# Neighbour sums of a graph layer: two fp32r halves against three bf16 parts and plain fp32 rows

## The chip, the cores and the metric

One core of a Trainium2 chip runs one program that holds four layers. The metric is device time in microseconds (us), the median of the runs. TensorE is shown as PE (matmuls) and PEld (weight loads), VectorE as DVE, ScalarE as ACT, GpSimd as POOL and SyncE as SP, which issues the plain transfers.

## The reference

The program normalises the 6250 x 256 features, adds a relational graph layer, an attention gate with four experts, a neighbour layer and a slice-attention layer. The change lies in the neighbour layer alone:

```
h_self   = feat @ W_self
h_sparse = keep the 32 largest of each row of feat @ W_neigh, the rest 0
summed   = segment_sum(h_sparse[src], dst)          # 200000 edges, sorted by dst
x        = x + h_self + summed / max(deg, 1)
```

feat is the row-normalised x. src is uniform over 6250 nodes; dst is dense at the low nodes and thin at the high ones. All is float32.

## The kernel before

Nodes stand in 49 windows of 128 rows. Two functions, run one after the other with a barrier of all engines at the end of each, make the neighbour layer.

**sparse_table** (L3012) makes the table of kept values. For each window ACT normalises the rows (norm, L3214), PE turns them (L3193) and ACT copies the turned rows out (copy, L3220); PE multiplies by both weights at once (L3202: plain fp32, 512 columns, of which 256 are h_self and 256 h_neigh). ACT takes the 512 columns out of PSUM (L3248, n_full). DVE searches the 32 largest in groups of four windows: four rounds of MAX8 (L3139) and MATCH_REPLACE8 (L3144). ACT makes a 0/1 mask of it (hide, L3228), seven windows behind its own loop. POOL adds h_self to x (L3113) and multiplies the mask by the values (choose, L3103, n_sparse). DVE cuts the upper 20 bits of each kept value out (head, L3152) and POOL subtracts them from the value (part, L3107): two halves that add up to the value exactly. SP writes n_sparse to table2 (1 KB a row) and the halves to table3 (2 KB a row).

Every engine works through its list in the written order. ACT's list for window w is norm(w+2), copy(w+1), hide(w-7), then the values of window w out of PSUM; DVE's is one group of four windows after the other, with the heads of four earlier windows between.

**neighbour_sums** (L1494) adds the rows up in two ways at once:

- The first 1024 tiles of 128 edges ("counted blocks") never fetch a row for an edge. Per pair of tiles (a group, 512 of them) DVE makes one-hots of source and target (mark, L1625 and L1627), PE multiplies them (outer, L1669, bf16) into a table of counts, ACT copies the counts into e_times (L1583), SP loads 128 neighbouring rows of table3 into e_loads (L1572), and PE multiplies counts by rows (inner, L1685). A group spans DWINDOWS = 1, 1, 2, 3, 3, 4, 5 or 5 windows of targets, and there is a matmul for each window and each half. Groups of a narrow and a wide block alternate, six windows to two groups throughout: 512 groups x 3 windows x 2 halves = 3072 matmuls of 256 columns.
- The other 544 tiles are gathered: POOL issues one indirect DMA a tile (L1600), 128 rows of table3 of 2 KB each, into a ring of 12 tiles; DVE makes a one-hot of targets (L1647), and PE multiplies it by both halves (L1697), two matmuls of 256 columns a tile.

PE's written order goes by gathered tile: the matmuls of tile t, then for the groups placed at it (groups_at, spread evenly over the first 528 tiles) outer(g) and inner(g-2). Operands of L1685 and L1697 are typed float32r ("fp32r"): one matmul instruction each, where a plain fp32 matmul shows as two. Four PSUM banks hold the running totals of a couple of blocks; between couples DVE adds them to the accumulators (take, L1639 and L1642), and PE clears the banks by multiplying zeros (L1679).

Of the kernel before, what the change touches and what calls it, by code (L numbers as in the profile page):

```python
# [5 lines left out]
F32 = mybir.dt.float32  # L6
I32 = mybir.dt.int32
BF16 = mybir.dt.bfloat16
# [73 lines left out]
UPPER = -(1 << 12)  # L82
# [1411 lines left out]
def neighbour_sums(nc, b, table, halves):  # L1494
# [7 lines left out]
    RING = 12  # L1502
# [33 lines left out]
    with Phase(nc) as ctx:  # L1536
        sem = lambda name: ctx.semaphore(name)
        sb = lambda name, shape, dt=F32: ctx.enter_context(nc.sbuf_tensor(name, shape, dt))
        ring = sb("e2_ring", [P, RING, 2, D], F32R)
        onehot = [sb(f"e2_onehot{s}", [P, P], F32R) for s in range(ONEHOTS)]  # L1540
# [5 lines left out]
        times = [sb(f"e2_times{s}", [P, DWIDE * P], F32R) for s in range(TIMES)]  # L1546
        loads = sb("e2_loads", [P, AHEAD, 2, D], F32R)
# [17 lines left out]
        @block_ctx.sync  # L1565
        def _(eng):
            for g in range(GROUPS):
                of = edges_of(g)
                at = of % (BLOCKS // 2) * P + of // (BLOCKS // 2)
                low = eng.value_load(b.dfirst[0:1, at:at + 1], min_val=0, max_val=NP - P)  # L1570
                wait_if(eng, spread, g - AHEAD + 1)
                eng.dma_start(loads[:, g % AHEAD, :, :].rearrange("p n d -> p (n d)").bitcast(F32),  # L1572
                              halves[bass.ds(low, P), :]).then_inc(fetched[g % AHEAD], 16)
            for s in range(AHEAD):
                eng.wait_ge(fetched[s], 16 * (GROUPS // AHEAD))
# [12 lines left out]
        @block_ctx.gpsimd  # L1588
        def _(eng):
            eng.iota(rampw[:, :], pattern=[[1, DWIDE * P]], base=0, channel_multiplier=0,  # L1590
                     allow_small_or_imprecise_dtypes=True).then_inc(numbered, 1)
            eng.iota(rampr[:, :], pattern=[[1, P]], base=0, channel_multiplier=0,
                     allow_small_or_imprecise_dtypes=True).then_inc(numbered, 1)
            eng.memset(zeros[:, :], 0.0).then_inc(numbered, 1)

            for t in range(TILES):
                if t >= RING:
                    eng.wait_ge(summed, t - RING + 1)
                    eng.sem_inc(cleared, 1)
                eng.indirect_dma_start(ring[:, t % RING, :, :].rearrange("p n d -> p (n d)").bitcast(F32), None, halves, bass.IndirectOffsetOnAxis(  # L1600
                    ap=b.esrc[:, FROM + t:FROM + t + 1], axis=0)).then_inc(gathered[t % RING], 16)
# [61 lines left out]
        def _(eng):  # L1663
# [10 lines left out]
            def inner(g):  # L1674
                n, c = block(g), g // COUPLE
                if g % COUPLE == 0:
                    wait_if(eng, taken, TAKEN_BY[c])
                    for s in banks[c]:
                        eng.matmul(total[s][:, :, :].rearrange("p w d -> p (w d)"), zeros[:, 0:P], zeros[:, :],  # L1679
                                   start=True, stop=False, skip_group_check=True)  # L1680
                eng.wait_ge(copied, units[g + 1])
                eng.wait_ge(fetched[g % AHEAD], 16 * (g // AHEAD + 1))
                for q in range(DWINDOWS[n]):
                    for half in range(2):
                        mm = eng.matmul(part(n, q), times[g % TIMES][:, q * P:(q + 1) * P],  # L1685
                                        loads[:, g % AHEAD, half, :], start=False, stop=False, skip_group_check=True)
# [1325 lines left out]
def sparse_table(nc, b, m):  # L3012
# [15 lines left out]
    with Phase(nc) as ctx:  # L3028
# [5 lines left out]
        full = [sb(f"n_full{s}", [P, 2, D]) for s in range(WAYS)]  # L3034
# [4 lines left out]
        split = [sb(f"n_split{s}", [P, 2, D]) for s in range(WAYS)]  # L3039
# [8 lines left out]
        upper = ctx.enter_context(nc.psum_tensor("n_upper", [P, BANK], F32))  # L3048
        bounded = sem("n_bounded")
# [13 lines left out]
        added = sem("n_added")  # L3063
        cleared = sem("n_cleared")
        stored = [sem(f"n_stored{s}") for s in range(WAYS)]
        headed = sem("n_headed")
        parted = sem("n_parted")
        block = ctx.enter_context(nc.Block())
        table = m["table2"].rearrange("(w p) d -> w p d", p=P)
        halves = m["table3"].rearrange("(w p) (n d) -> w p n d", p=P, n=2)  # L3070

        @block.sync
        def _(eng):
# [11 lines left out]
            def body(few):  # L3085
                for w, q in few:
                    eng.wait_ge(chosen, w + 1)
                    eng.dma_start(table[w], sparse[q][:, :]).then_inc(stored[q], 16)
                    eng.wait_ge(headed, w + 1)
                    eng.wait_ge(parted, w + 1)  # L3090
                    eng.dma_start(halves[w], split[q][:, :, :]).then_inc(stored[q], 16)
# [7 lines left out]
        def _(eng):  # L3099
            def choose(w):  # L3100
                eng.wait_ge(masked, w + 1)
                wait_if(eng, stored[w % WAYS], 32 * (w // WAYS))
                eng.tensor_tensor(sparse[w % WAYS][:, :], mask[w % WAYS][:, :], full[w % WAYS][:, 1, :], ALU.mult).then_inc(chosen, 1)  # L3103

            def part(w):
                eng.wait_ge(headed, w + 1)
                eng.tensor_tensor(split[w % WAYS][:, 1, :], sparse[w % WAYS][:, :], split[w % WAYS][:, 0, :],  # L3107
                                  ALU.subtract).then_inc(parted, 1)

            eng.memset(less[:, :], -1.0).then_inc(cleared, 1)  # L3110
            for w in range(NW):
                eng.wait_ge(evacuated, w + 1)
                eng.tensor_tensor(b.x[:, w, :], b.x[:, w, :], full[w % WAYS][:, 0, :], ALU.add).then_inc(added, 1)  # L3113
                if w >= LATER:
                    choose(w - LATER)
                if w >= LATER + BEHIND:
                    part(w - LATER - BEHIND)
            for w in range(NW - LATER, NW):
                choose(w)
                part(w - BEHIND)  # L3120
            for w in range(NW - BEHIND, NW):
                part(w)
            eng.wait_ge(chosen, NW)
            eng.wait_ge(parted, NW)
            eng.wait_ge(added, NW)

        @block.vector
        def _(eng):
            def search(few):
# [3 lines left out]
                for r in range(ROUNDS):  # L3133
                    values = lambda q: full[q][:, 1, :] if r == 0 else left[q][:, :]
# [14 lines left out]
            def head(w):  # L3149
                eng.wait_ge(chosen, w + 1)  # L3150
                wait_if(eng, stored[w % WAYS], 32 * (w // WAYS))
                eng.tensor_tensor(split[w % WAYS][:, 0, :].bitcast(I32), sparse[w % WAYS][:, :].bitcast(I32),  # L3152
                                  upper[:, 0:D].bitcast(I32), ALU.bitwise_and).then_inc(headed, 1)

            def pair(i):
# [3 lines left out]
                if not isinstance(i, int) or i > 0:  # L3159
                    for w in range(WAYS * i - GROUP4, WAYS * i):  # L3160
                        head(w)
                search(here(GROUP4))
                for w in range(WAYS * i, WAYS * i + GROUP4):
                    head(w)
# [3 lines left out]
            eng.memset(upper[:, 0:D].bitcast(I32), UPPER).then_inc(bounded, 1)  # L3168
# [5 lines left out]
            eng.wait_ge(bounded, 1)  # L3174
# [4 lines left out]
            for w in range(NW - 1 - GROUP4, NW):  # L3179
                head(w)  # L3180
# [8 lines left out]
        def _(eng):  # L3189
# [6 lines left out]
            def body(w, s):  # L3196
# [14 lines left out]
        def _(eng):  # L3211
# [18 lines left out]

            eng.wait_ge(stated, STATED)
# [6 lines left out]
            for w in range(NW):  # L3238
# [8 lines left out]
                wait_if(eng, added, w - WAYS + 1)  # L3247
                eng.activation(full[w % WAYS][:, :, :].rearrange("p n d -> p (n d)"), product[w % 2][:, :],  # L3248
                               ACT.Copy).then_inc(evacuated, 1)
            for w in range(NW - LATER, NW):  # L3250
                hide(w)
# [494 lines left out]
def build(nc, m):  # L3746
# [3 lines left out]
    m["table3"] = nc.dram_tensor("table3", [NP, 2 * D], F32).ap()  # L3750
# [124 lines left out]
```

## Time and profile before

| | |
|---|---|
| time, median of 3 runs | 4351.2 us (4351.14 to 4359.82) |
| span of the profiled execution | 4349.6 us, mean granted clock 0.906 |
| sparse_table | 3010 to about 3195 us |
| neighbour_sums | about 3196 to 3951 us |
| PE busy over the span | 3703.0 us (85%) |
| moved by DMA over the span | 682.83 MB, mean 157 GB/s |

The profiled execution has no time of its own beside its span; the median of the runs is 1.6 us longer than the span, and what is added to the span is added to the median. Matmuls are pipelined: a matmul's duration in a row is longer than the distance to the next one, and it is the distance that says how many fit into a microsecond. A merged row of a timeline (x10) lasts from the first start to the last end.

### The profile page before, as it was taken

The page shows a single profiled execution, that of the slowest core. Times are in us where ns is not written, and L with a number is a line of the kernel's source. Part 1 is how long each engine was busy: PE and PEld are TensorE (multiplying, and loading weights), DVE is VectorE, ACT ScalarE, POOL GpSimd, SP SyncE. Part 2 cuts the span into 40 slices and gives each one's busy share as a digit, 9 for nine tenths or more (in the row PEclk, how much of TensorE's full clock was granted, in tenths as well). Part 3 has the DMA queues.
Part 4 walks back from the last instruction along what each step waited for, and adds up shares of the span by engine and source line. Part 5 has one row for each costly group of instructions (what it writes and reads, how often), then busy time and mean ns, then how long its engine had stood idle before and what let it go on. Part 6 is the DMA issues. An engine that isn't in the chain of part 4 may idle for free. (4 is left out here: it accounts for less than half of the span.)

```text
span 4349.6 us, 73406 instructions
## 1 busy us (share of the span) xinstructions
PE 3703.0 (85%) x19616; PEld 2744.7 (63%) x19641; DVE 2690.5 (62%) x9486; ACT 1684.8 (39%) x3943; POOL 2823.1 (65%) x2869
## 2 busy tenths in 40 slices
PE   4999996778777778877699999978769999996988
PEld 2566663444445556746588888866348888884657
DVE  8766656656544443445555455557978888886862
ACT  3444453434323333323344444446523333333320
POOL 5777777777777777772577777751667767672230
PEclk9999997776689999975799999999879999997998
DMA  7555553333434443531423323336379999993001
GB/s 252 188 193 186 188 191 119 105 105 105 115 115 124 125 123 106 164 105 43 91 66 69 69 66 70 70 101 213 117 279 385 368 367 385 373 385 95 1 1 59
DMA packets 354620, 682.83 MB, mean 157 GB/s; under 512 B 69218, under 2 KB 181104, under 8 KB 347853
## 3 DMA queue, kind: packets, MB, share of 16 engines
q0 software_dynamic: 133184, 338.60, 25.7%
q1 hardware_dynamic: 221039, 339.52, 23.1%
q8 instruction: 178, 2.92, 0.3%
q14 instruction: 219, 1.79, 0.1%
HBM read 565.53 MB, written 112.35 MB: 156 GB/s over the span
## 5 line engine op out<-in xcount | busy, mean ns | idle before, releaser
L1070 POOL DMA_INDIRECT e_ring<-table,erow x1040 | 1004.6, 966 | 316.9 <-issue 165.2
L1488 PE MATMUL e_sums<-e_ring,e_onehot 128*128 128x257 f32 x2080 | 821.2, 501 | 297.4 <-DMA e_ring<-table,erow 250.4
L2587 POOL DMA_INDIRECT t_source<-source_rows,t_index x632 | 606.9, 960 | 209.0 <-issue 157.2
L1488 PEld LDWEIGHTS e_sums<-e_ring,e_onehot 128*128 128x128 f32 x2080 | 379.7, 226 | 564.5 <-issue 332.6
L1600 POOL DMA_INDIRECT e_ring<-table,esrc x544 | 531.1, 976 | 212.9 <-issue 128.3
L560 POOL DMA_INDIRECT r_ring<-rows,esrc x400 | 449.7, 1124 | 149.7 <-issue 93.0
L1036 ACT ACTIVATE k_sign<-ramp,low 128x128 bf16<-128x128 f32 x1024 | 364.1, 395 | 447.9 <-PE e_sums L1459 429.7
L1685 PE MATMUL e_total<-e_loads,e_times 128*128 128x256 f32 x3072 | 502.7, 300 | 17.2 <-DMA e_loads<-table 12.3
L1685 PEld LDWEIGHTS e_total<-e_loads,e_times 128*128 128x128 f32 x3072 | 409.3, 190 | 69.5 <-issue 35.2
L1583 ACT ACTIVATE e_times<-e_tally 128x320 fp32r<-128x320 f32 (+4 forms) x640 | 259.7, 426 | 484.8 <-PE e_tally L1669 480.0
L2771 PE MATMUL t_raw<-big,t_w 128*128 128x256 f32 x1600 | 377.9, 390 | 20.2 <-ACT t_hidden L2606 19.4
L1305 DVE SCALAR_TENSOR_TENSOR big<-e_sums,within,big 128x257 f32 x130 | 63.0, 484 | 532.8 <-PE e_sums L1488 530.4
L738 PE MATMUL r_product<-weights,r_xt 128*128 128x512 f32 x784 | 372.0, 597 | 0.0
L2782 PE MATMUL t_out<-t_w,t_hidden 128*128 128x256 f32 x1600 | 368.2, 383 | 0.0
L2771 PEld LDWEIGHTS t_raw<-big,t_w 128*128 128x128 f32 x1600 | 301.8, 193 | 65.8 <-ACT t_hidden L2606 26.1
L1627 DVE TENSOR_SCALAR e_place<-e_rampw,ddst 128x128 bf16<-128x128 f16 (+4 forms) x1024 | 340.0, 334 | 0.0
L1625 DVE TENSOR_SCALAR e_row<-e_rampr,dsrc 128x128 bf16<-128x128 bf16 x1024 | 272.8, 268 | 95.9 <-PE e_tally L1669 84.5
L2782 PEld LDWEIGHTS t_out<-t_w,t_hidden 128*128 128x128 f32 x1600 | 297.7, 190 | 37.3
L1367 DVE TENSOR_SCALAR e_onehot<-ramp,edst 128x128 f32<-128x128 f32 x1040 | 247.0, 295 | 18.0 <-DVE d_keys L1092 2.2
L1669 PE MATMUL e_tally<-e_place,e_row 128*128 128x320 bf16 (+4 forms) x1258 | 255.4, 300 | 1.5
L1697 PE MATMUL e_sums<-e_ring,e_onehot 128*128 128x256 f32 x1088 | 202.0, 284 | 44.7 <-DMA e_ring<-table,esrc 44.6
L752 PE MATMUL r_sums<-r_ring,r_onehot 128*128 128x257 f32 x800 | 220.1, 385 | 19.2 <-DMA r_ring<-rows,esrc 19.1
(560 smaller groups left out, 6336.4 us busy)
## 6 DMA issues: line engine op xcount, KB each, us to landing
e_loads<-table SPq DMA_DIRECT2D x512, 256.0 KB
table<-r_stage SPq DMA_DIRECT2D x49, 1024.0 KB
outputs<-first_outputs SPq DMA_DIRECT2D x49, 512.0 KB, 6.6
first_outputs<-t_stage SPq DMA_DIRECT2D x96, 256.0 KB
t_near<-near_rows SPq DMA_DIRECT2D x79, 256.0 KB
e_ring<-table,erow POOLq DMA_INDIRECT x1040
table<-n_split SPq DMA_DIRECT2D x49, 256.0 KB
t_source<-source_rows,t_index POOLq DMA_INDIRECT x632
```

The lines of the kernel that those rows point to most:

```text
L560: eng.indirect_dma_start(ring[:, t % RING, 0:D], None, m["rows1"], bass.IndirectOffsetOnAxis(ap=b.esrc[:, SKIP + t:SKIP + t + 1], axis=0)) ...
L738: mm = eng.matmul(product[n % BANKS][:, :], xt[w % 2][:, k, :], b.weights[:, k, 2 * c:2 * c + 2, :].rearrange("p r o -> p (r o)"), start=( ...
L1036: eng.activation(sign[t % SIGNS][:, :], b.ramp[:, 0:P], ACT.Sign, bias=b.low[:, t:t + 1], scale=1.0).then_inc(signed, 1)
L1070: eng.indirect_dma_start(ring[:, t % RING, 0:D], None, table, bass.IndirectOffsetOnAxis(ap=b.erow[:, EARLY + t:EARLY + t + 1], axis=0)).th ...
L1488: eng.matmul(sums[g % SUMS][:, 0:ACCW], onehot[t % ONEHOTS][:, :], ring[:, t % RING, :], start=(t % GROUP == 0), stop=(t % GROUP == GROUP ...
L1600: eng.indirect_dma_start(ring[:, t % RING, :, :].rearrange("p n d -> p (n d)").bitcast(F32), None, halves, bass.IndirectOffsetOnAxis(ap=b. ...
L1625: eng.tensor_scalar(row[g % (MARKS // 2)][:, two, :], rampr[:, :], b.dsrc[:, column(tile):column(tile) + 1], None, ALU.is_equal).then_inc( ...
L1627: eng.tensor_scalar(place[(2 * g + two) % MARKS][:, 0:wide(g) * P], rampw[:, 0:wide(g) * P], b.ddst[:, column(tile):column(tile) + 1], Non ...
L1685: mm = eng.matmul(part(n, q), times[g % TIMES][:, q * P:(q + 1) * P], loads[:, g % AHEAD, half, :], start=False, stop=False, skip_group_ch ...
L2587: eng.indirect_dma_start(source[s][:, q, :], None, a.source_rows, bass.IndirectOffsetOnAxis(ap=index[s][:, q:q + 1], axis=0)).then_inc(gat ...
L2771: mm = eng.matmul(raw[g][:, j % 2, :], w1[:, e, k, j * P:(j + 1) * P], b.xt[:, k, bass.ds(w * P, PAIR)], start=(k == 0), stop=(k == KH - 1))
L2782: mm = eng.matmul(out[s][:, q, :], hidden[s][:, j, q * P:(q + 1) * P], w2[:, e, j, :], start=(j == 0), stop=(j == NB - 1))
```

## The change

The table for the neighbour sums is stored as three bf16 parts (first the value rounded to bf16, then the rest rounded, then what is left; 1.5 KB a row) in place of two fp32 halves. Counted blocks load these parts and multiply counts in bf16 by three parts. Gathered tiles take plain fp32 rows of table2 (1 KB) and plain fp32 one-hots: one fp32 matmul a tile. The ring has 24 tiles of 1 KB rows in place of 12 of 2 KB.

In sparse_table the parts are made by two ACT copies to bf16 (head, middle) and two POOL subtractions (remain, last); DVE's heads and POOL's addition to x are gone. x is added by PE instead (a matmul of the identity by x into the product's first 256 columns), and ACT takes the product out of PSUM in two pieces, one into x and one into n_full.

```diff
 def neighbour_sums
-    RING = 12
+    RING = 24
-        ring = sb("e2_ring", [P, RING, 2, D], F32R)
-        onehot = [sb(f"e2_onehot{s}", [P, P], F32R) for s in range(ONEHOTS)]
+        ring = sb("e2_ring", [P, RING, D])
+        onehot = [sb(f"e2_onehot{s}", [P, P]) for s in range(ONEHOTS)]
-        times = [sb(f"e2_times{s}", [P, DWIDE * P], F32R) for s in range(TIMES)]
-        loads = sb("e2_loads", [P, AHEAD, 2, D], F32R)
+        times = [sb(f"e2_times{s}", [P, DWIDE * P], BF16) for s in range(TIMES)]
+        loads = sb("e2_loads", [P, AHEAD, THIRDS, D], BF16)
...
-                eng.indirect_dma_start(ring[:, t % RING, :, :]..., None, halves, ...
+                eng.indirect_dma_start(ring[:, t % RING, :], None, table, ...
...
-                    for half in range(2):
+                    for third in range(THIRDS):
                         mm = eng.matmul(part(n, q), times[g % TIMES][:, q * P:(q + 1) * P],
-                                        loads[:, g % AHEAD, half, :], start=False, stop=False, skip_group_check=True)
+                                        loads[:, g % AHEAD, third, :], start=False, stop=False, skip_group_check=True)
...
-                for half in range(2):
-                    mm = eng.matmul(sums[g8 % 2][:, 0:D], onehot[t % ONEHOTS][:, :], ring[:, s, half, :],
-                                    start=(half == 0 and t % GROUP == 0), stop=(half == 1 and t % GROUP == GROUP - 1))
-                mm.then_inc(summed, 1)
+                eng.matmul(sums[g8 % 2][:, 0:D], onehot[t % ONEHOTS][:, :], ring[:, s, :],
+                           start=(t % GROUP == 0), stop=(t % GROUP == GROUP - 1)).then_inc(summed, 1)
 def sparse_table
         # gpsimd
-            for w in range(NW):
-                eng.wait_ge(evacuated, w + 1)
-                eng.tensor_tensor(b.x[:, w, :], b.x[:, w, :], full[w % WAYS][:, 0, :], ALU.add).then_inc(added, 1)
-                if w >= LATER:
-                    choose(w - LATER)
-                if w >= LATER + BEHIND:
-                    part(w - LATER - BEHIND)
+            for w in range(NW + 2):
+                if w < NW:
+                    choose(w)          # also waits for first of w - WAYS
+                if 1 <= w <= NW:
+                    remain(w - 1)      # rest = sparse - parts[0], waits for first
+                if w >= 2:
+                    last(w - 2)        # parts[2] = rest - parts[1], waits for second
         # vector: head(w) and its calls in pair(i) and at the end are gone
         # tensor, body(w, s)
                 wait_if(eng, evacuated, w - 1)
+                wait_if(eng, kept, w - 1)
                 for k in range(KH):
                     mm = eng.matmul(product[s][:, :], xt[s][:, k, :], ...
+                    if k == 0:
+                        eng.matmul(product[s][:, 0:D], b.ident[:, :], b.x[:, w, :], start=False, stop=False)
         # scalar
+            def head(w):
+                eng.wait_ge(chosen, w + 1)
+                wait_if(eng, stored[w % WAYS], 32 * (w // WAYS))
+                eng.activation(parts[w % WAYS][:, 0, :], sparse[w % WAYS][:, :], ACT.Copy).then_inc(first, 1)
+            def middle(w):
+                eng.wait_ge(rested, w + 1)
+                eng.activation(parts[w % WAYS][:, 1, :], rest[w % len(rest)][:, :], ACT.Copy).then_inc(second, 1)
+            def split(w):              # where in range: hide(w), head(w - 1), middle(w - 2)
...
-                if w >= LATER:
-                    hide(w - LATER)
+                split(w - LATER)
                 eng.wait_ge(multiplied, w + 1)
                 wait_if(eng, chosen, w - WAYS + 1)
-                eng.activation(full[w % WAYS][:, :, :]..., product[w % 2][:, :], ACT.Copy).then_inc(evacuated, 1)
+                eng.activation(b.x[:, w, :], product[w % 2][:, 0:D], ACT.Copy).then_inc(kept, 1)
+                eng.activation(full[w % WAYS][:, :], product[w % 2][:, D:2 * D], ACT.Copy).then_inc(evacuated, 1)
-            for w in range(NW - LATER, NW):
-                hide(w)
+            for w in range(NW - LATER, NW + 2):
+                split(w)
 def build
-    m["table3"] = nc.dram_tensor("table3", [NP, 2 * D], F32).ap()
+    m["table3"] = nc.dram_tensor("table3", [NP, THIRDS * D], BF16).ap()
```

## Rows read from the trace of the kernel before

**Rows 1.** The page: busy us (share of the span) of each engine; DMA busy tenths

```profile
PE 3703.0 (85%) x19616; PEld 2744.7 (63%) x19641; DVE 2690.5 (62%) x9486; ACT 1684.8 (39%) x3943; POOL 2823.1 (65%) x2869
...
DMA  7555553333434443531423323336379999993001
```

**Rows 2.** Busy us by stretch: PE, PEld, DVE, ACT, POOL; PE clock, DMA share, GB/s

```profile
3010.00:3195.50 185.50, 115.46 (x294) 50.38 (x294) 163.01 (x649) 87.85 (x198) 103.52 (x148) 0.83 0.34 122
...
3202.40:3946.60 744.20, 709.91 (x5428) 615.80 (x5452) 621.33 (x2729) 259.73 (x640) 527.17 (x541) 0.99 1.02 372
```

**Rows 3.** Groups in 3202.4 to 3946.6 us: busy us, mean ns, idle before, releasers

```profile
L1600 POOL DMA_INDIRECT e_ring<-table,esrc x541 | 527.6, 975 | 212.1 <-issue 127.6 <-PE e_sums L1697 84.5
L1685 PE MATMUL e_total<-e_loads,e_times 128*128 128x256 f32 x3072 | 502.7, 300 | 17.2 <-DMA e_loads<-table 12.3 <-ACT e_times L1583 3.2
L1685 PEld LDWEIGHTS e_total<-e_loads,e_times 128*128 128x128 f32 x3072 | 409.3, 190 | 69.5 <-issue 35.2 <-ACT e_times L1583 17.1
...
L1697 PE MATMUL e_sums<-e_ring,e_onehot 128*128 128x256 f32 x1088 | 202.0, 284 | 44.7 <-DMA e_ring<-table,esrc 44.6
```

**Rows 4.** Timeline of PE around 3351 us: start, us, line, count

```profile
3350.19 1.46 PE L1685 MATMUL e_total<-e_loads,e_times 128*128 128x256 f32 x10
3351.49 0.64 PE L1697 MATMUL e_sums<-e_ring,e_onehot 128*128 128x256 f32 x4
3351.97 0.29 PE L1669 MATMUL e_tally<-e_place,e_row 128*128 128x128 bf16 x2
3352.07 0.48 PE L1685 MATMUL e_total<-e_loads,e_times 128*128 128x256 f32 x2
3352.39 0.74 PE L1669 MATMUL e_tally<-e_place,e_row 128*128 128x320 bf16 x4
3352.86 1.46 PE L1685 MATMUL e_total<-e_loads,e_times 128*128 128x256 f32 x10
```

**Rows 5.** Timeline of PE elsewhere: fp32 of 256 columns, bf16 of 20, 512 and 384

```profile
2508.52 3.62 PE L2782 MATMUL t_out<-t_w,t_hidden 128*128 128x256 f32 x16
...
2511.97 0.75 PE L2758 MATMUL gsums<-t_parts,t_place 128*128 128x20 bf16 x24
...
3758.40 0.82 PE L1679 MATMUL e_total<-e_zeros 128*128 128x512 bf16 x3 [2.95 <-DVE big L1642]
...
1298.82 0.49 PE L1444 MATMUL d_keys<-d_target,d_half 128*128 128x384 bf16 x2
```

**Rows 6.** One line's durations, ns min/median/max: L1444, L2782

```profile
L1444 PE MATMUL d_keys<-d_target,d_half x128: 322/326/528, 1235.2 to 1639.2; 128*128 128x384 bf16 x128
...
L2782 PE MATMUL t_out<-t_w,t_hidden x1600: 378/379/463, 2123.2 to 2911.1; 128*128 128x256 f32 x178
```

**Rows 7.** Groups in 3010 to 3195.5 us: busy us, mean ns, idle before, releasers

```profile
L3144 DVE MATCH_REPLACE8 n_left<-n_best,n_left 128x256 f32<-128x256 f32 x147 | 58.5, 409 | 0.0
...
L3214 ACT ACTIVATE n_xn<-features,shift,rstd 128x256 f32<-128x256 f32 x49 | 28.8, 590 | 0.8 <-DVE shift L3173 0.8
L3228 ACT ACTIVATE n_mask<-n_left,n_less 128x256 f32<-128x256 f32 x49 | 24.3, 503 | 60.8 <-DVEq L3147 60.8
...
L3220 ACT ACTIVATE n_xt<-n_turned 128x256 f32<-128x256 f32 x49 | 18.2, 371 | 1.2 <-PE n_turned L3194 1.2
...
L3152 DVE TENSOR_TENSOR n_split<-n_sparse,n_upper 128x256 int32<-128x256 int32 x49 | 17.3, 414 | 2.5 <-DVE n_left L3144 2.0 <-POOL n_sparse L3103 0.2
```

**Rows 8.** Timeline of DVE and ACT in sparse_table: start, us, line, count

```profile
3154.10 1.41 DVE L3152 TENSOR_TENSOR n_split<-n_sparse,n_upper 128x256 int32<-128x256 int32 x4 [0.22 <-DVE n_left L3144]
...
3167.26 1.41 DVE L3152 TENSOR_TENSOR n_split<-n_sparse,n_upper 128x256 int32<-128x256 int32 x4 [0.22 <-DVE n_left L3144]
...
3168.59 1.40 DVE L3139 MAX8 n_best<-n_full 128x8 f32<-128x256 f32 x4
...
3179.11 1.71 ACT L3228 ACTIVATE n_mask<-n_left,n_less 128x256 f32<-128x256 f32 x4 [9.21 <-DVEq L3147]
```

More of the change, by code:

```diff
@@ L81 @@
 TAKEN = -2.0 ** 127
-UPPER = -(1 << 12)
+THIRDS = 3
 SH, SD, SG = 8, 64, 64
@@ L1491, in _, with neighbour_sums @@
                     tally(t)
-def neighbour_sums(nc, b, table, halves):
+def neighbour_sums(nc, b, table, thirds):
     ONEHOTS = BODY
-    RING = 12
+    RING = 24
     MARKS = 8
@@ L1571, in _ @@
                 wait_if(eng, spread, g - AHEAD + 1)
-                eng.dma_start(loads[:, g % AHEAD, :, :].rearrange("p n d -> p (n d)").bitcast(F32),
-                              halves[bass.ds(low, P), :]).then_inc(fetched[g % AHEAD], 16)
+                eng.dma_start(loads[:, g % AHEAD, :, :].rearrange("p n d -> p (n d)"),
+                              thirds[bass.ds(low, P), :]).then_inc(fetched[g % AHEAD], 16)
             for s in range(AHEAD):
@@ L1599, in _ @@
                     eng.sem_inc(cleared, 1)
-                eng.indirect_dma_start(ring[:, t % RING, :, :].rearrange("p n d -> p (n d)").bitcast(F32), None, halves, bass.IndirectOffsetOnAxis(
+                eng.indirect_dma_start(ring[:, t % RING, :], None, table, bass.IndirectOffsetOnAxis(
                     ap=b.esrc[:, FROM + t:FROM + t + 1], axis=0)).then_inc(gathered[t % RING], 16)
@@ L3033, in sparse_table @@
         xt = [sb(f"n_xt{s}", [P, KH, P]) for s in range(2)]
-        full = [sb(f"n_full{s}", [P, 2, D]) for s in range(WAYS)]
+        full = [sb(f"n_full{s}", [P, D]) for s in range(WAYS)]
         left = [sb(f"n_left{s}", [P, D]) for s in range(WAYS)]
@@ L3038, in sparse_table @@
         sparse = [sb(f"n_sparse{s}", [P, D]) for s in range(WAYS)]
-        split = [sb(f"n_split{s}", [P, 2, D]) for s in range(WAYS)]
+        parts = [sb(f"n_parts{s}", [P, THIRDS, D], BF16) for s in range(WAYS)]
+        rest = [sb(f"n_rest{s}", [P, D]) for s in range(WAYS // 2)]
         less = sb("n_less", [P, 1])
@@ L3047, in sparse_table @@
         product = [ctx.enter_context(nc.psum_tensor(f"n_product{s}", [P, BANK], F32)) for s in range(2)]
-        upper = ctx.enter_context(nc.psum_tensor("n_upper", [P, BANK], F32))
-        bounded = sem("n_bounded")
         loaded = sem("n_loaded")
@@ L3062, in sparse_table @@
         chosen = sem("n_chosen")
-        added = sem("n_added")
+        kept = sem("n_kept")
         cleared = sem("n_cleared")
         stored = [sem(f"n_stored{s}") for s in range(WAYS)]
-        headed = sem("n_headed")
-        parted = sem("n_parted")
+        first = sem("n_first")
+        rested = sem("n_rested")
+        second = sem("n_second")
+        third = sem("n_third")
         block = ctx.enter_context(nc.Block())
         table = m["table2"].rearrange("(w p) d -> w p d", p=P)
-        halves = m["table3"].rearrange("(w p) (n d) -> w p n d", p=P, n=2)
+        thirds = m["table3"].rearrange("(w p) (n d) -> w p n d", p=P, n=THIRDS)
         @block.sync
@@ L3088, in body @@
                     eng.dma_start(table[w], sparse[q][:, :]).then_inc(stored[q], 16)
-                    eng.wait_ge(headed, w + 1)
-                    eng.wait_ge(parted, w + 1)
-                    eng.dma_start(halves[w], split[q][:, :, :]).then_inc(stored[q], 16)
+                    eng.wait_ge(second, w + 1)
+                    eng.wait_ge(third, w + 1)
+                    eng.dma_start(thirds[w], parts[q][:, :, :]).then_inc(stored[q], 16)
             each_few(eng, body)
@@ L3101, in choose, with remain, last @@
                 eng.wait_ge(masked, w + 1)
+                wait_if(eng, first, w - WAYS + 1)
                 wait_if(eng, stored[w % WAYS], 32 * (w // WAYS))
[L3103 to L3108, printed above, removed]
-            eng.memset(less[:, :], -1.0).then_inc(cleared, 1)
-            for w in range(NW):
-                eng.wait_ge(evacuated, w + 1)
-                eng.tensor_tensor(b.x[:, w, :], b.x[:, w, :], full[w % WAYS][:, 0, :], ALU.add).then_inc(added, 1)
-                if w >= LATER:
-                    choose(w - LATER)
-                if w >= LATER + BEHIND:
-                    part(w - LATER - BEHIND)
-            for w in range(NW - LATER, NW):
[L3119 to L3125, printed above, removed]
+                eng.tensor_tensor(sparse[w % WAYS][:, :], mask[w % WAYS][:, :], full[w % WAYS][:, :], ALU.mult).then_inc(chosen, 1)
+            def remain(w):
+                eng.wait_ge(first, w + 1)
+                wait_if(eng, third, w - len(rest) + 1)
+                eng.tensor_tensor(rest[w % len(rest)][:, :], sparse[w % WAYS][:, :], parts[w % WAYS][:, 0, :],
+                                  ALU.subtract).then_inc(rested, 1)
+            def last(w):
+                eng.wait_ge(second, w + 1)
+                eng.tensor_tensor(parts[w % WAYS][:, 2, :], rest[w % len(rest)][:, :], parts[w % WAYS][:, 1, :],
+                                  ALU.subtract).then_inc(third, 1)
+            eng.memset(less[:, :], -1.0).then_inc(cleared, 1)
+            for w in range(NW + 2):
[5 more added lines that the diff above has]
+                    last(w - 2)
+            eng.wait_ge(third, NW)
         @block.vector
@@ L3133, in search @@
                 for r in range(ROUNDS):
-                    values = lambda q: full[q][:, 1, :] if r == 0 else left[q][:, :]
+                    values = lambda q: full[q][:, :] if r == 0 else left[q][:, :]
                     for w, q in few:
@@ L3147, in search @@
                     eng.sem_inc(searched, 1)
[L3149 to L3153, printed above, removed]
             def pair(i):
@@ L3158, in pair @@
                 search(here(0))
-                if not isinstance(i, int) or i > 0:
-                    for w in range(WAYS * i - GROUP4, WAYS * i):
-                        head(w)
                 search(here(GROUP4))
-                for w in range(WAYS * i, WAYS * i + GROUP4):
-                    head(w)
             s = Chain(eng, stated)
             variances(eng, s, b, b.counts, work)
-            eng.memset(upper[:, 0:D].bitcast(I32), UPPER).then_inc(bounded, 1)
             eng.wait_ge(rooted, 1)
@@ L3173, in _ @@
             r.did(eng.scalar_tensor_tensor(b.shift[:, :], b.mean[:, :], -1.0, b.rstd[:, :], ALU.mult, ALU.mult))
-            eng.wait_ge(bounded, 1)
             pair(0)
@@ L3178, in _ @@
             search([(NW - 1, 0)])
-            for w in range(NW - 1 - GROUP4, NW):
-                head(w)
             eng.wait_ge(brought, 128)
@@ L3229, in hide @@
                                scale=-2.0 ** -126).then_inc(masked, 1)
+            def head(w):
[6 more added lines that the diff above has]
+            def split(w):
+                if w >= 0 and w < NW:
+                    hide(w)
+                if w - 1 >= 0 and w - 1 < NW:
+                    head(w - 1)
+                if w - 2 >= 0 and w - 2 < NW:
+                    middle(w - 2)
             eng.wait_ge(stated, STATED)
@@ L3242, in _ @@
                     copy(w + 1)
-                if w >= LATER:
-                    hide(w - LATER)
+                split(w - LATER)
                 eng.wait_ge(multiplied, w + 1)
                 wait_if(eng, chosen, w - WAYS + 1)
[L3247 to L3250, printed above, removed]
-                hide(w)
+                eng.activation(b.x[:, w, :], product[w % 2][:, 0:D], ACT.Copy).then_inc(kept, 1)
+                eng.activation(full[w % WAYS][:, :], product[w % 2][:, D:2 * D], ACT.Copy).then_inc(evacuated, 1)
+            for w in range(NW - LATER, NW + 2):
+                split(w)
+            eng.wait_ge(kept, NW)
 def attention_phase(nc, b, m):
```

## The prediction

> **What bounds the kernel now.** I read the page first: PE is the busiest engine (85%), and DMA is full in the fourth quarter of the span alone [rows 1]. That quarter is the neighbour sums, so the stretches come next [rows 2]. In the 744.2 us from the first to the last matmul of that stage PE is shown busy for 710, DMA for 102% at 372 GB/s, DVE for 621, POOL for 527 and ACT for 260. Two things look full, so the question is which of them the stage would keep if the other were relieved. The idle times say little against PE: it waited 17 us for loads and counts, and 45 us for gathered rows, of which some 38 lie ahead of the first one [rows 3]. The timeline settles it. One turn of PE's list, two groups with two gathered tiles, runs from 3350.19 to 3352.86 without a shown wait, 2.67 us [rows 4]. There are 256 such turns, with 528 tiles between them (2.06 a turn), and 16 tiles behind the last. At 0.24 us for a tile's two matmuls (four in 0.48, from 3351.49 to 3351.97) that is 256 x (2.67 + 0.0625 x 0.24) = 687, and 4 for the last tiles: 691 of 744 us are PE's own issue. The other 53 are waits: about 5 at the start, 3 at each of the three changes of couple (one stands in the rows [rows 5]: 2.95 us for DVE ahead of the zeros), 8 in the last tiles, and some 31 scattered ones.
>
> So transfers and PE are nearly level, PE slightly ahead. In sparse_table it is DVE: 163 of 185 us [rows 2], in groups of four windows 13.16 us apart (3154.10 to 3167.26) [rows 8].
>
> **Counted blocks.** Per turn six windows get three matmuls in place of two: 18 for 12, of 256 columns each. The old ones go at 0.119 us: four of the same shape last 0.64 with a last one of 0.284, (0.64 - 0.28) / 3 [rows 3, 4]. A bf16 matmul of 256 columns behind another is what the trace of before doesn't show in such a run, so I bound it. Below: a pair of 384 columns lasts 0.49 with a second of 0.326, 0.164 apart [rows 5, 6], which is 0.43 ns a column, or 0.109 for 256. Above: 0.12, no better than the fp32r matmuls that it replaces. Which end holds hangs on the weights, loaded anew for each matmul. An fp32r load takes 0.190 [rows 3] and sits beside every 0.119 step; the bf16 matmuls of 20 columns, each with its load, follow at (0.75 - 0.17) / 23 = 0.025 [rows 5] (0.17 for the last one), so bf16 loads need not slow a 0.109 step. I take 0.109 and keep 0.12 as the upper end. Per turn 18 x 0.109 - 12 x 0.119 = +0.53 us, over 256 turns +137 (at 0.12: +187).
>
> The Trainium skill, "TensorE: Matmul & The Clock Gate", section "Back-to-back issue gap", has a warm gap of columns / 2.4 GHz plus 2.5 ns, 109 ns here, but also says that streams of weight load and matmul are set by both. With its first figure the sum is the same; its caution is what the upper end stands for.
>
> **Gathered tiles.** A plain fp32 matmul is two instructions: 16 of them, 256 columns wide, last 3.62 with a last one of 0.379, (3.62 - 0.38) / 15 = 0.216 apart [rows 5, 6]. A tile costs 0.432 for 0.238, +0.194, and 544 tiles +105 us. This price is the trace's own; I give it no spread.
>
> **What gets cheaper.** Bytes: 512 loads fall from 256 to 192 KB (134 to 101 MB) and 544 gathers from 256 to 128 KB (143 to 71 MB), 172 for 277 MB. Over a stage that is longer, DMA stands under half. Of the 53 us of waits, the scattered 31 go almost entirely, I leave 3; the 8 in the last tiles go, since PE then takes 0.43 us a tile with 24 of them fetched ahead; start and couple changes stay. So minus 36. POOL issues as many gathers: 528 busy and 128 of issue for 541 [rows 3], 1.21 us each, 659 us in all, no bound under a longer stage, and nor are DVE's 621 or ACT's 260. ACT's copies of counts keep their number and shape.
>
> Sum for the stage: 744 + 137 + 105 - 36 = 950, **+206 us**. Nothing of another stage lies beside it (a barrier on both sides), so all of it reaches the end.
>
> **The table stage.** DVE's four heads a group go: from 3167.26 to 3168.59 1.33 us, with 0.22 of wait ahead [rows 8], 1.55 a group, 17 us for eleven groups; the five at the end (0.33 each) stood before POOL's last parts, and I count 1. Whether DVE can use it depends on ACT's list, which grows by two copies of SBUF rows (near L3228: 0.503 long, (1.71 - 0.50) / 3 = 0.40 apart) and one more PSUM copy (L3220: 0.371) [rows 7, 8]. Per window that is at most 0.59 + 0.37 + 3 x 0.50 + 2 x 0.37 = 3.2 us by whole durations, some 2.5 by distances; DVE's group without heads is 11.6, 2.9 a window. The wait that matters: behind hide (which waits for the first window of a search to end) now stand head, middle and the copy into x before the last window of the next group gets out of PSUM, 0.50 + 0.40 + 0.40 + 0.30 + 0.37 = 2.0 us. DVE meanwhile has three more replaces (0.41 each, [rows 7]) and three MAX8 (0.35 each, from four in 1.40 [rows 8]), 2.3 us, so about 0 to 0.3 of wait a group, I take 2 us in all. At the start PE paces the first four windows, and the identity matmul adds 2 x 0.216 to each: +2. POOL trades three operations for three. At the end ACT's hide of the last window stands ahead of head and middle of the two before, a chain of six short steps against POOL's five queued parts before; I call it even. SP stores smaller parts, two transfers a window as before. The other new waits are met earlier: PE's for the copy into x by its wait for n_full, which ACT fills right after; POOL's choose waits for a head eight windows back, with choose, remain and last queued behind it. Together **-14 us**, between -20 and +10.
>
> Span 4349.6 + 206 - 14 = 4541.6, and with the 1.6 us by which the median of the runs exceeds the span, **4543 us**.
>
> **Rival 1: bf16 steps of 0.12.** Then 18 x 0.011 x 256 = 51 us more, 4594. For it: each matmul has weights of its own, and the steps in this very stage are 0.12 [rows 4]. Against it: the 384-column pair and the 20-column run. 24%.
>
> **Rival 2: the stage is bound by transfers and gets faster.** For it: DMA at 102% [rows 2]. If bytes alone set the time, 172 MB at 372 GB/s are 462 us; POOL's 659 us would then end last, with 10 of start and end a stage of 669, -75, and with the table stage 4351 - 75 - 14 = 4262. Against it: 691 us of issue. It decides only where a turn's matmuls fit into 2.6 us; with 0.72 for the tallies (2.67 less 12 x 0.119 and 0.48) and 2 x 0.43 for the tiles, a bf16 matmul would have to take (2.6 - 0.72 - 0.86) / 18 = 0.057 us, half of 0.109. 4%.
>
> The Trainium skill, "DMA: Bandwidth & Descriptors", section "Specifications", puts a core's HBM limit near 358 GB/s. The stage measured 372, so by that rule it is at the ceiling, and cutting bytes is what would pay; that is this rival's reading. [...]
>
> **Rival 3: the table stage becomes ACT's.** If ACT's activations follow each other by whole durations, a group takes 4 x 3.2 = 12.8 and the 2.0 us chain no longer hides: 15 us for 13.16, +22 over twelve groups in place of -14, 4579. Against it: four hides in 1.71 us [rows 8]. 9%.
>
> **How the numbers follow.** Forecast 62%, its own range 4518 to 4565 (no scattered waits and -20 in the table; 10 us more of waits and 0 there, with a step between the two bounds). With rivals 1 and 3 the range is 4515 to 4608, which leaves out rival 2 and the far ends, under 2 in 10. 0.2% is about what a measurement of this kernel can tell from no change. Faster is rival 2, 4%; no case lands within 0.2%, 1% for what I haven't thought of; slower 95%.
>
> **What would show it.** In the changed profile: L1685's counterpart x4608 at 0.109 in runs of 15 between two others; the gathered tiles x1088 as fp32, 0.216 apart; DMA share in the stage near one half; POOL waiting for PE at most gathers, its ring full; DVE's idle time in front of its one-hots or marks, put down to PE; the stage some 950 us from first to last matmul. In the table stage: groups 11.6 to 12 us apart, no int32 operation on DVE. A stage under 900 us, or PE waiting for e_ring or e_loads throughout, would make the prediction wrong, as would a bf16 step well under 0.1 us.

## The result and the profile after

The changed kernel takes 4515.66 us (median of 4 runs, 4514.36 to 4518.29), the kernel before 4351.17 in the same set: a ratio of 1.0375, 95% interval 1.0362 to 1.0387, 164 us slower. The forecast was 4543, 192 slower. The direction came out as forecast, and none of the three rivals did; the size is 27 us off. The measured time lies at the very low end of the range, 4515, and its interval reaches to 4509.

The page of the changed kernel, the lines that answer to [rows 1]: busy us by engine, and DMA's busy tenths in 40 slices.

```profile
PE 3933.8 (87%) x21239; PEld 2892.8 (64%) x21275; DVE 2675.8 (59%) x9436; ACT 1716.6 (38%) x4090; POOL 2807.3 (62%) x2869
...
DMA  7555553333444433523232333363666666672001
```

The nines of DMA in the fourth quarter have become sixes. The two stretches of [rows 2] in the changed kernel, busy us of PE, PEld, DVE, ACT and POOL, clock, DMA share and GB/s:

```profile
3010.00:3182.00 172.00, 126.09 (x392) 67.00 (x392) 147.06 (x599) 119.25 (x345) 97.49 (x148) 0.88 0.33 113
3188.30:4109.30 921.00, 910.73 (x6953) 735.54 (x6988) 624.93 (x2733) 259.22 (x640) 520.54 (x542) 1.00 0.65 188
```

From the first to the last matmul the neighbour sums take 921 us for 744, +177 where +206 was forecast. DMA moves half of the former GB/s, but is still busy for 0.65 of the time, where the working had it under half; PE is busy for 911 of 921. The groups that answer to [rows 3] (busy us, mean ns, idle before and its releasers):

```profile
L1685 PE MATMUL e_total<-e_loads,e_times 128*128 128x256 bf16 x4608 | 586.9, 273 | 0.0
L1600 POOL DMA_INDIRECT e_ring<-table,esrc x542 | 521.0, 961 | 380.0 <-PE e_sums L1696 283.0 <-issue 97.0
L1685 PEld LDWEIGHTS e_total<-e_loads,e_times 128*128 128x128 bf16 x4608 | 445.9, 98 | 84.8 <-issue 0.6
L1696 PE MATMUL e_sums<-e_ring,e_onehot 128*128 128x256 f32 x1088 | 306.7, 381 | 32.9 <-DMA e_ring<-table,esrc 32.9
```

PE never waits for loads or counts (0.0), and for a gathered row only ahead of the first tile (one wait of 32.9). POOL waits for PE 283 us in all: its ring is full. One turn of PE's list, to be laid beside [rows 4] (start, us, line, count):

```profile
3302.49 0.71 PE L1669 MATMUL e_tally<-e_place,e_row 128*128 128x320 bf16 x4
3303.03 1.80 PE L1685 MATMUL e_total<-e_loads,e_times 128*128 128x256 bf16 x15
3304.67 1.03 PE L1696 MATMUL e_sums<-e_ring,e_onehot 128*128 128x256 f32 x4
3305.54 0.28 PE L1669 MATMUL e_tally<-e_place,e_row 128*128 128x128 bf16 x2
3305.65 0.49 PE L1685 MATMUL e_total<-e_loads,e_times 128*128 128x256 bf16 x3
3305.98 0.71 PE L1669 MATMUL e_tally<-e_place,e_row 128*128 128x320 bf16 x4
```

From one group of tallies to the next, 3302.49 to 3305.98, a turn is 3.49 us, where the working gave 2.67 + 0.53 + 0.39 = 3.59. The bf16 step is (1.80 - 0.27) / 14 = 0.109, the fp32 one (1.03 - 0.38) / 3 = 0.217: both prices were right. So this tenth of a microsecond must lie in what was left at its old price. It is missing in the turns of the first two couples of blocks; those of the last two are a case of their own, taken up further down.

In the table stage the searches of DVE follow each other without heads (start, us; to be laid beside [rows 8]):

```profile
3145.02 1.41 DVE L3138 MAX8 n_best<-n_full 128x8 f32<-128x256 f32 x4 [0.29 <-DVE n_left L3143]
...
3156.92 1.41 DVE L3138 MAX8 n_best<-n_full 128x8 f32<-128x256 f32 x4 [0.28 <-DVE n_left L3143]
```

A group takes 11.90 us for 13.16, and the profile puts DVE's wait down to its own replaces, not to ACT. By the first and the last instruction the stage is 169.3 us for 180.4, -11 where -14 was forecast. With +177 in the sums and some 3 us less over barriers and other stages that is the 163.1 by which the span grew.

### The profile page after: what moved, and what is told of

The parts are those of the page before. It is cut to its first block and busy times, and to the rows that moved or that the text cites. A ratio compares the mean times of both kernels' runs of the same rounds, so it can differ in the third digit from the quotient of the medians.

```text
span 4512.7 us, 76792 instructions
## 1 busy us (share of the span) xinstructions
PE 3933.8 (87%) x21239; PEld 2892.8 (64%) x21275; DVE 2675.8 (59%) x9436; ACT 1716.6 (38%) x4090; POOL 2807.3 (62%) x2869
## 5 line engine op out<-in xcount | busy, mean ns | idle before, releaser
L1488 PE MATMUL e_sums<-e_ring,e_onehot 128*128 128x257 f32 x2080 | 838.0, 510 | 279.7 <-DMA e_ring<-table,erow 233.5
L1685 PE MATMUL e_total<-e_loads,e_times 128*128 128x256 bf16 x4608 | 586.9, 273 | 0.0
L1583 ACT ACTIVATE e_times<-e_tally 128x320 bf16<-128x320 f32 (+4 forms) x640 | 259.2, 425 | 661.4 <-PE e_tally L1669 658.4
L1685 PEld LDWEIGHTS e_total<-e_loads,e_times 128*128 128x128 bf16 x4608 | 445.9, 98 | 84.8 <-issue 0.6
L1696 PE MATMUL e_sums<-e_ring,e_onehot 128*128 128x256 f32 x1088 | 306.7, 381 | 32.9 <-DMA e_ring<-table,esrc 32.9
L1627 DVE TENSOR_SCALAR e_place<-e_rampw,ddst 128x128 bf16<-128x128 f16 (+4 forms) x1024 | 327.9, 321 | 0.0
L1669 PE MATMUL e_tally<-e_place,e_row 128*128 128x320 bf16 (+4 forms) x1248 | 245.3, 293 | 1.8
```

The source lines that it names most:

```text
L1488: eng.matmul(sums[g % SUMS][:, 0:ACCW], onehot[t % ONEHOTS][:, :], ring[:, t % RING, :], start=(t % GROUP == 0), stop=(t % GROUP == GROUP ...
L1627: eng.tensor_scalar(place[(2 * g + two) % MARKS][:, 0:wide(g) * P], rampw[:, 0:wide(g) * P], b.ddst[:, column(tile):column(tile) + 1], Non ...
```

## The experiments

**Gathered tiles alone.** The kernel before with one part of the change:

```diff
 # kernel before, neighbour_sums
-    RING = 12
+    RING = 24
-        ring = sb("e2_ring", [P, RING, 2, D], F32R)
+        ring = sb("e2_ring", [P, RING, D])
-        onehot = [sb(..., [P, P], F32R) ...]
+        onehot = [sb(..., [P, P]) ...]
         # gather from table in place of halves; one fp32 matmul a tile in place of two fp32r
```

> The kernel before with the gathered tiles alone as in the changed kernel: plain fp32 rows of 1 KB, fp32 one-hots, ring of 24; counted blocks keep their fp32r halves. Theory (PE's issue bounds the stage): a tile's matmuls go from 0.238 to 0.432 us, 544 x 0.194 = +105, and some 36 us of waits go with the bytes (205 for 277 MB) and the deeper ring: 4420 us. If the waits of the kernel before were not made by transfers, only the 8 us of the last tiles go: 4448. If transfers bounded the stage before (rival 2), the stage follows bytes down to PE's new issue of about 796 and no further: also near 4420, but then DMA, not PE, must have been what the stage before waited for; the run with half loads tells these apart.

Measured: 4397.24 us, ratio 1.0109 (1.0094 to 1.0123), +49. The stretch from the first to the last matmul of its sums:

```profile
3196.60:3992.60 796.00, 788.24 (x5451) 670.66 (x5452) 621.34 (x2731) 259.98 (x640) 518.29 (x541) 0.99 0.84 259
```

The stretch is 796 us for 744. The theory's +69 is too much by 20. Either more waits went than the 36 counted, or the tiles cost less than 105; with the next run the two can be told apart.

**Half of the loads.** The kernel before, moving less and multiplying as much:

```diff
 # kernel before, neighbour_sums
-        loads = sb("e2_loads", [P, AHEAD, 2, D], F32R)
+        loads = sb("e2_loads", [P, AHEAD, D], F32R)
-                eng.dma_start(loads[:, g % AHEAD, :, :]..., halves[bass.ds(low, P), :])
+                eng.dma_start(loads[:, g % AHEAD, :].bitcast(F32), table[bass.ds(low, P), :])
-                                        loads[:, g % AHEAD, half, :], ...
+                                        loads[:, g % AHEAD, :], ...
```

> The kernel before with loads of 128 KB in place of 256 for the counted blocks (rows of the whole values, the same 1 KB multiplied twice): the same matmuls, 210 for 277 MB. The counted sums come out doubled and unsplit. Theory: PE issues as before, 691 us, and only the scattered waits that transfers made can go: 15 to 31 us, 4320 to 4336. Rival (transfers bound the stage before): the stage falls to POOL's 659 and some 16 at the ends, 4282. Rival (the scattered waits are PE's own or ACT's): under 5 us, 4347 or more.

Measured: 4312.10 us, ratio 0.9914 (0.9902 to 0.9927), -36. Stretch and the group of the counted matmuls:

```profile
3194.30:3903.00 708.70, 692.08 (x5452) 622.91 (x5452) 616.58 (x2732) 259.64 (x640) 530.15 (x542) 0.98 0.91 297
```

```profile
L1685 PE MATMUL e_total<-e_loads,e_times 128*128 128x256 f32 x3072 | 509.6, 302 | 0.0
```

The stage stands at 709, not at 675: PE's issue was the wall behind the transfers, and transfers cost 35 us in front of it (15 to 31 were expected here, and the prediction let 28 of the scattered waits go). Rival 2 falls.

This run and the one before it move about as much (210 and 205 MB), so between them lies the price of the gathered tiles: 796.0 - 708.7 = +87, the shorter tail taken in (forecast: 105 - 8 = 97). By the starts of the matmuls in the two traces the tiles themselves cost the full 105; the waits in the last tiles shrink by some 12 and not 8, and the tally pairs behind a tile by 5 (the run with fp32r below takes these up). From the kernel with gathered fp32 tiles to the changed one lies the price of the counted blocks: 921 - 796 = +125 (forecast: 137).

**Two of three parts.** The changed kernel, a third of the counted matmuls left out:

```diff
 # changed kernel, inner
-                    for third in range(THIRDS):
+                    for third in range(2):
```

> The changed kernel with the third part left out of the multiplication (it is still made, stored and loaded): 3072 bf16 matmuls for 4608. Leaves out the lowest part of the values of the counted blocks. Theory: 1536 x 0.109 = 168 us less, 4348, the stage 753 us, since POOL's 659 and DVE's 621 stay below. Rival (something else stands close behind PE, ACT's copies of counts or POOL's issue): less falls away, 4370 or more, with PE waiting for e_times or e_ring.

Measured: 4355.39 us, ratio to the kernel before 1.0016 (1.0007 to 1.0025), so 160 below the changed kernel in place of 168. Its sums and the one new wait:

```profile
3182.30:3944.30 762.00, 754.03 (x5451) 586.34 (x5452) 620.66 (x2731) 259.16 (x640) 519.40 (x542) 0.99 0.76 226
```

```profile
PEld e_tally L1669 <- ACT e_times L1583: 18.9, 69, 0.5
```

921 - 762 = 159. The 1536 matmuls are worth 0.104 us each, nearly their whole step. Most of the other 9 us are a wait that stood behind: with a shorter inner the tallies of a wide block catch up with ACT's copies (18.9 us in 69 waits, where the changed kernel has 11.8 in 70), and turns are 2.83 or 2.94 us long. The rival is right about a neighbour close behind PE, and wrong about its size.

**What fp32r does to its neighbours.** The changed kernel with one fp32r matmul a tile:

```diff
 # changed kernel, neighbour_sums
-        ring = sb("e2_ring", [P, RING, D])
-        onehot = [sb(f"e2_onehot{s}", [P, P]) for s in range(ONEHOTS)]
+        ring = sb("e2_ring", [P, RING, D], F32R)
+        onehot = [sb(f"e2_onehot{s}", [P, P], F32R) for s in range(ONEHOTS)]
```

> The changed kernel with rows and one-hots of the gathered tiles typed float32r, so that a tile is one matmul at that precision instead of a plain fp32 one; leaves out the lower bits of the gathered values. Theory (an fp32r matmul makes the matmuls around it dearer): the tallies that follow a gathered tile show 0.067, 0.120 and 0.173 for 128, 256 and 384 columns between the two of a pair, as in the kernel before, where the changed kernel has 0.056, 0.109 and 0.162; the tile itself 0.12 in place of 0.432; 544 x 0.31 = 170 less and 5 to 10 back, 4351 to 4356. Rival (the dearer tallies of the kernel before came from its heavier transfers): tallies stay at 0.056, 0.109 and 0.162, 4346.

Measured: 4359.60 us, ratio to the kernel before 1.0021 (1.0012 to 1.0031). What decides is the distance between the starts of the two matmuls of a tally pair (outer makes one for each of a group's two tiles; the median of all 128, 64 and 128 pairs of a trace, in ns; L1669, bf16):

| columns | before | half loads | gathered fp32 | changed | gathered fp32r |
|---|---|---|---|---|---|
| 128 | 67 | 67 | 56 | 56 | 67 |
| 256 | 120 | 120 | 109 | 109 | 120 |
| 384 | 173 | 173 | 162 | 162 | 173 |
| what runs ahead of the pair | fp32r | fp32r | fp32 | fp32 | fp32r |

Eleven ns come and go with the type of the matmul ahead of the pair, not with the transfers: half the loads change nothing, and the last column has them back at the bytes of the changed kernel. Where bf16 runs ahead (the version with two bf16 parts, below) it is 56, 109 and 162 again. The pair itself starts on time, 122 ns after a tile's last fp32r matmul in the kernel before and 216 after its last fp32 one in the changed kernel, so the 11 ns are added to the turn. The dearer neighbours are shown. The median turn of this run, 2.88 us, is what these prices give (3.49 - 2 x 0.312 + 0.022 = 2.89); the total is 4 to 8 us above what was expected, so that lies in waits, which I haven't traced.

**The ring.** The changed kernel with 12 tiles:

```diff
-    RING = 24
+    RING = 12
```

> The changed kernel with a ring of 12 tiles in place of 24. Theory (PE's issue ends last and gathers are early): no difference, 4515 within 4. Rival (the deeper ring covers late gathers, above all in the last 16 tiles): 5 to 15 us more, PE waiting for e_ring.

Measured: 4517.63 us, ratio to the kernel before 1.0379 (1.0361 to 1.0397), against 1.0375: in the total, no difference that can be told. The trace does show the rival's wait, though. PE waits for gathered rows four times, and in the changed kernel once:

```profile
  DMA e_ring<-table,esrc: 34.8, 4
```

The three new waits (0.8, 1.5 and 1.0 us) stand ahead of the last four tiles, and the matmuls behind the last counted one take some 5 us longer; from first to last matmul the stage is 928 us for 921, while the whole span is 3.9 longer. So the deeper ring does cover late gathers at the end, as the prediction had it; the medians of the runs, 2 us apart with ranges that overlap, don't show it.

**The table stage alone.** The kernel before, with DVE's cut moved to ACT and the sums as they were:

```diff
 # kernel before, sparse_table
-        split = [sb(f"n_split{s}", [P, 2, D]) for s in range(WAYS)]
+        split = [sb(f"n_split{s}", [P, 2, D], F32R) for s in range(WAYS)]
         # vector: head(w) and its calls are gone
+            def head(w):               # scalar, called one window behind hide
+                eng.wait_ge(chosen, w + 1)
+                wait_if(eng, stored[w % WAYS], 32 * (w // WAYS))
+                eng.activation(split[w % WAYS][:, 0, :], sparse[w % WAYS][:, :], ACT.Copy).then_inc(headed, 1)
         # x added by PE's identity matmul, PSUM taken out in two pieces, as in the changed kernel
         # gpsimd: choose(w), then part(w - 1)
```

> The kernel before with the table stage alone changed: ACT rounds the kept values into the upper half (typed float32r) in place of DVE's cut, POOL subtracts as before, and x is added by PE's identity matmul. The neighbour sums are untouched. Theory (DVE bounds the table stage): 11 to 14 us less, 4338 to 4340, faster than both kernels. Rival (ACT's longer list takes over): no gain or up to 20 us more.

Measured: 4334.98 us, ratio 0.9964 (0.9951 to 0.9977), -13.5: faster than both kernels, with the values still split into two halves that add up to them. Its searches:

```profile
3143.93 1.41 DVE L3131 MAX8 n_best<-n_full 128x8 f32<-128x256 f32 x4 [0.29 <-ACT n_full L3238]
...
3155.83 1.41 DVE L3131 MAX8 n_best<-n_full 128x8 f32<-128x256 f32 x4 [0.28 <-ACT n_full L3238]
```

A group takes 11.90 us, as in the changed kernel, which makes one ACT copy and one POOL operation a window more. The profile puts the wait down to ACT here and to DVE there, but it is 0.28 to 0.29 us in both, whatever the length of ACT's list. So neither ACT nor POOL sets the distance of the groups; rival 3 falls. Behind the start of the last search, though, this kernel needs 7.6 us to the end of the stage, the changed one 11.3 and the kernel before 10.0.

**Two bf16 parts everywhere.** The changed kernel with a cheaper split:

```diff
 # changed kernel
-THIRDS = 3
+THIRDS = 2
-        ring = sb("e2_ring", [P, RING, D])
-        onehot = [sb(f"e2_onehot{s}", [P, P]) for s in range(ONEHOTS)]
+        ring = sb("e2_ring", [P, RING, THIRDS, D], BF16)
+        onehot = [sb(f"e2_onehot{s}", [P, P], BF16) for s in range(ONEHOTS)]
         # gathers fetch both parts (1 KB a row); two bf16 matmuls a tile; POOL's last(w) is gone
```

> The changed kernel with two bf16 parts in place of three, everywhere: rows of 1 KB with two parts for counted blocks and gathered tiles alike, bf16 one-hots, two bf16 matmuls a tile, POOL's second subtraction gone. Keeps some 16 bits of each summed value, where three parts keep 24. Theory: a turn of PE's list is that of the run without the third part (2.83 to 2.94 us) with 2 x 0.218 for the tiles in place of 2 x 0.432, 2.41 to 2.51, in all 617 to 643 and 4 for the last tiles; POOL's issue, 544 x 1.21 = 659 and some 16 at the ends, then ends last: stage 675 to 690, time 4270 to 4290, with POOL no longer waiting for PE. Rival (the steps of PE still end last, or DVE's 621 of marks in the way): stage 700 to 720, 4300 to 4320.

Measured: 4290.40 us, ratio 0.9857 (0.9839 to 0.9876), -61. It is the fastest version, at the price of bits: some 16 of each value for 24. Stretch and POOL's list in it (start, us):

```profile
3183.70:3883.00 699.30, 651.29 (x5427) 512.37 (x5452) 612.14 (x2734) 259.46 (x640) 529.69 (x542) 0.98 0.70 199
```

```profile
3401.48 0.97 POOL L1600 DMA_INDIRECT e_ring<-table,esrc  x1 [0.31 <-issue]
3402.75 0.94 POOL L1600 DMA_INDIRECT e_ring<-table,esrc  x1 [0.30 <-issue]
3404.00 0.95 POOL L1600 DMA_INDIRECT e_ring<-table,esrc  x1 [0.30 <-issue]
```

POOL issues without a real wait, 1.25 us a gather, and PE now waits for its rows throughout (us in all, times, longest):

```profile
POOL e_ring L1600 <- PE e_sums L1697: 35.7, 117, 0.3
PE e_sums L1697 <- DMA e_ring<-table,esrc: 31.7, 41, 2.2
PEld e_sums L1697 <- DVE e_onehot L1647: 24.5, 28, 2.4
```

What the profile puts down to POOL waiting for PE is never longer than the 0.3 us that lie between any two issues. So POOL is the next wall, as worked out; that DVE, whose one-hots some weight loads wait for, has a part in it isn't ruled out. The stage is 699 for 675 to 690, since 544 x 1.25 are 680 and not 659 (the 1.21 of the working was a mean over issue times, some of which the profile puts down to waits for PE); from POOL's first issue to its last, 3180.5 to 3877.3, it is 1.28 each, as some issues last longer than the 0.95 of these rows.

## Why the prediction was right or wrong

- **What bounds the stage** was right in kind: PE's issue stands behind the transfers, and relieving the transfers alone gave 35 us. How much of the 744 us was issue, and how much was waiting, was not right (below).
- **The bf16 step** of 0.109 was right, and the choice between it and 0.12 with it. Rival 1 would have been 51 us more. Of the two statements of the Trainium skill (TensorE: Matmul & The Clock Gate, section Back-to-back issue gap) the trace agrees with the first, columns over the clock and a little, which is 109 ns here; what it adds, that in a stream with weight loads both set the step, changes nothing here: 15 such matmuls, each with its load, hold 0.109.
- **The fp32 step** of 0.216 was right, read off another stage.
- **The first step that failed** is "256 x (2.67 + 0.0625 x 0.24) = 687", and with it the waits, "minus 36". A turn of 2.67 us was read in the first couple of blocks and taken for all four. In the third couple of the kernel before, one group of 256-column tallies follows the other after 2.58 us:

```profile
3600.35 0.39 PE L1669 MATMUL e_tally<-e_place,e_row 128*128 128x256 bf16 x2
...
3602.93 0.39 PE L1669 MATMUL e_tally<-e_place,e_row 128*128 128x256 bf16 x2
```

  The median turns of the four couples are 2.667, 2.667, 2.580 and 2.573 us, and within 1 ns the same with half of the loads, so this is issue and not waiting. 64 times their sum is 671, and 8 for the tiles between and behind them make 679 us of issue, not 691, and 65 of waits, not 53. In the changed kernel the medians are 3.490, 3.490, 3.483 and 3.483: 892.5 and 13.8 for the tiles, 906 us of issue and 15 of waits. So 50 us of waits went where 36 were counted.
- **The second step that failed** is "18 x 0.109 - 12 x 0.119" and the tile's "0.432 for 0.238", with everything else in a turn left as it was. Issue grew by 906 - 679 = 227 us where 137 + 105 = 242 were forecast. Two terms were put at nothing. The tally pairs lose 11 ns each with the fp32r matmuls ahead of them (the table above; 0.147 to 0.136 for 320 columns, 0.226 to 0.216 for 512), 7 us over 640 pairs. And a counted run after a pair of 128 columns started late: from the second of that pair to the second of the run 0.229 us before, 0.165 after, of which 0.01 is the run's own step; 128 times some 0.054 is 7 us. Behind wider pairs only the step's own 0.01 is gone. The first was switched on and off by a run. The second goes with the type of the counted matmuls: 0.229 with half of the loads and with gathered fp32 too, 0.165 with gathered fp32r too; no run changes it alone. What weight load stands behind it is an argument: an fp32r one takes 0.190 in [rows 3], longer than the 0.134 that two steps of such a pair take; no run shows it as the cause.
- Together: 227 - 50 = +177 for the forecast +206. The two misses, 15 and 14 us, point the same way.
- **The table stage**: -11 for -14. The distances of the groups gave 13.7 us, for 17 less 2 of wait in the working; the start cost 1.4 for 2. The rest is the end, called even with 1 us saved: from the start of the last search the stage lasts 11.3 us for 10.0. With two halves in place of three parts (the run on the table stage) it is 7.6.
- **The range**: the low end of the forecast's own range, 4518, does not follow from what stands beside it: no scattered waits (3 us) and -20 in the table (6 us) give 4534. That the result lies at 4515 and not far below it is owed to slack that no term carries. No term allowed the removed matmuls to be dearer than their best step, or a turn to differ between couples.
- Two smaller readings: the tallies of Rival 2 are 2.67 - 12 x 0.119 - 0.48 = 0.76 and not 0.72, which changes nothing (0.054 for 0.057). And the 372 GB/s that its reading takes for a ceiling is a mean: the same stage moves 385 from 3600 to 3700 us.

## What to carry to other kernels

Price what a change removes in place, from the distance between what stands ahead of it and what stands behind it, and not from the best step inside a run: here the neighbours of the removed instructions got cheaper too. Read a turn in every part of the schedule before multiplying it by the number of turns; issue that is put too high hides waits that a change will free. Where two resources look full, work out the issue time of each by itself: moving a quarter less (210 for 277 MB) was worth 35 us of 744, and the change, which moves 38% less, added 227 us of issue. And a split into more, narrower parts pays only if a part's step is enough shorter than the step that it replaces: three bf16 matmuls of 0.109 don't beat two fp32r ones of 0.12.

## What the runs showed of the hardware

A bf16 pair of 128, 256 or 384 columns takes 11 ns more between its starts when an fp32r matmul runs ahead of it than when a plain fp32 or a bf16 one does (67, 120, 173 against 56, 109, 162 ns), at either level of transfers. A run of fp32r matmuls behind a bf16 pair of 128 columns reaches its second matmul 0.229 us after the second of the pair, a run of bf16 ones 0.165. bf16 matmuls of 256 columns, each with a weight load of its own, hold 0.109 us over runs of 15. A row of an fp32r matmul behind a bf16 one begins early: in the kernel before the first counted matmul is shown starting 29 ns after a tally of 320 columns, where the next bf16 matmul in the changed kernel starts after 136, so a run's first distance must be read together with the tally ahead of it.
